# A chain of eight stages on one core: operands of later stages brought and split ahead of their stage

## The reference

```python
x = layernorm(x + L0_attn(x))   # tanh recurrence over 256 steps, 16 heads of state 64
x = layernorm(x + L0_ffn(x))    # router, 8 experts, top 2, gelu
x = layernorm(x + L1_attn(x))   # keys with rope, latent queries, softmax over 128-token chunks
x = layernorm(x + L1_ffn(x))    # router with bias, 64 experts in groups, top 6, gated silu
x = layernorm(x + L2_attn(x))   # gated linear attention, log-sigmoid decay
x = layernorm(x + L2_ffn(x))    # router with bias, 160 experts, top 8, silu
x = layernorm(x + L3_attn(x))   # 6 transformer layers with linear attention, own weights each
x = layernorm(x + L3_ffn(x))    # layer norm with gain, then attention with heads of 16
```

## Time and profile before

| | |
|---|---|
| median of 3 runs | 2036.42 us (2035.14 to 2037.17) |
| profiled execution, its time | 2036.34 us |
| its span, first to last instruction | 2034.6 us |
| PE busy | 1728.0 us, 85% |
| DVE busy | 1585.6 us, 78% |
| ACT busy | 1251.1 us, 61% |
| POOL busy | 348.9 us, 17% |
| mean granted TensorE clock | 0.871 |

### The profile page before, as it was taken

One profiled execution on the slowest core, in us unless ns is written; L12 is line 12 of the kernel. 1 busy time (PEld: TensorE's weight loads), 2 busy tenths in 40 slices (PEclk: granted clock), 3 DMA queues, 4 the chain that ended last, 5 costly groups with the idle time before them and its releaser, 6 DMA issues. The chain is left out here.

```text
span 2034.6 us, 46173 instructions
## 1 busy us (share of the span) xinstructions
PE 1728.0 (85%) x16491; PEld 1083.0 (53%) x16498; DVE 1585.6 (78%) x3793; ACT 1251.1 (61%) x3209; POOL 348.9 (17%) x464
## 2 busy tenths in 40 slices
PE   5999969846859999947759999999968999999585
PEld 5999944435633444425544444444436666665453
DVE  4444459878878999967878999999967787777774
ACT  5666637723526655555438888888856666665465
POOL 1000001000011111110001212222113443443211
PEclk7555569978968999978989999999979999999798
DMA  3000007210004443300006666666620000000100
GB/s 79 10 4 4 4 15 271 88 43 1 0 14 171 154 171 149 141 17 1 0 12 232 232 232 225 224 226 229 232 87 22 22 1 22 21 1 1 36 2 22
DMA packets 51670, 174.06 MB, mean 86 GB/s; under 512 B 7104, under 2 KB 32448, under 8 KB 34112
## 3 DMA queue, kind: packets, MB, share of 16 engines
q1 hardware_dynamic: 50368, 170.09, 23.3%
q10 hardware_dynamic: 1152, 1.90, 0.3%
HBM read 167.45 MB, written 2.95 MB: 84 GB/s over the span
## 5 line engine op out<-in xcount | busy, mean ns | idle before, releaser
L861 DVE TENSOR_TENSOR ps<-ps,m_comb 128x512 f32<-128x512 f32 x520 | 363.1, 699 | 23.9 <-DMA m_comb<-m_shares 7.2
L846 DVE TENSOR_TENSOR m_hwlo<-ps,m_hwhi 128x512 f16<-128x512 f32 x520 | 353.5, 680 | 0.3
L822 ACT ACTIVATE m_hwhi<-ps 128x512 f16<-128x512 f32 x520 | 308.3, 593 | 20.8 <-DVE ps L861 19.4
L828 ACT ACTIVATE ps<-ps 128x512 f32<-128x512 f32 x388 | 225.9, 582 | 80.7 <-PE ps L778 80.5
L778 PE MATMUL ps<-x_hi,m_whi 128*128 128x512 f16 x652 | 250.3, 384 | 8.2 <-DVE m_hwlo L846 4.2
L778 PE MATMUL ps<-x_lo,m_whi 128*128 128x512 f16 x652 | 250.0, 383 | 0.0
L778 PE MATMUL ps<-x_hi,m_wlo 128*128 128x512 f16 x652 | 249.7, 383 | 0.0
L759 POOL CAST m_whi<-m_stage 128x256 f16<-128x256 f32 (+1 forms) x130 | 55.2, 424 | 907.2 <-PE ps L784 637.6
L461 DVE TENSOR_TENSOR rn_s_lo<-rn_s_full,rn_s_hi 128x32 f16<-128x32 f32 x512 | 98.4, 192 | 131.5 <-ACT rn_s_full L418 131.5
L784 PE MATMUL ps<-m_hwhi,m_whi 128*128 128x512 f16 x520 | 197.4, 380 | 0.3 <-DVE m_hwlo L846 0.2
L784 PE MATMUL ps<-m_hwlo,m_whi 128*128 128x512 f16 x520 | 197.3, 379 | 0.0
(11 more groups left out here) (451 smaller groups left out, 3983.8 us busy)
## 6 DMA issues: line engine op xcount, KB each, us to landing
m_comb<-m_shares SPq DMA_DIRECT2D x128, 1024.0 KB, 5.1
m_stage<-in_m_w SPq DMA_DIRECT2D x97, 128.0 KB, 4.6
m_stage<-in_m_w SPq DMA_DIRECT2D x33, 192.0 KB, 4.7
lj_w<-in_lj_w SPq DMA_DIRECT2D x6, 1024.0 KB, 5.1
lq_w<-in_lq_w SPq DMA_DIRECT2D x1, 1600.0 KB, 6.9
la_w<-in_la_w SPq DMA_DIRECT2D x1, 1280.0 KB, 5.3
rn_rows<-in_L_attn_rows SPq DMA_DIRECT2D x4, 256.0 KB, 4.5
rn_xs<-rn_xn_hi SPq DMA_DIRECT2D x32, 32.0 KB, 1.9
```

The lines of the kernel that those rows point to most:

```text
L822: nc.scalar.activation(hw_hi[:, k % HB, :], weighted(k), ACT.Copy).then_inc(hi_done, 1)
L828: nc.scalar.activation(acted(k), ps[:, 4, :] if gated else bank(k), func).then_inc(act_done, 1)
L846: nc.vector.tensor_tensor(hw_lo[:, k % HB, :], weighted(k), hw_hi[:, k % HB, :], ALU.subtract)\
L861: nc.vector.tensor_tensor(weighted(k), bank(k), comb[:, s, n * QW:(n + 1) * QW], ALU.mult)\
```

## The change

Tiles that last over several stages are made in `build`. Two routers' tiles last from start to end. An early group holds the other routers' weights and all operands of `l1_attn` and `l2_attn`, with room for the split parts; it is closed before stage 5 (`l2_ffn`). A late group then holds the first weights of `l3_attn` and the operands of `l3_ffn`. Nothing that is computed changes.

- All early tiles are requested by SP at the end of its list in `l0_attn` (15 transfers, 2.6 MB), behind the recurrence's own.
- `l0_ffn`'s POOL list gets four instructions at its end: the cast and subtraction of `la_w` (2560 columns) and of `lg_w` (772).
- `l2_ffn`'s SP list gets 7 transfers, 2.9 MB (`lj_w` of layer 0, `lj_cols`, `lj_own`, `lq_w`, `lq_cols`, `lq_vb`, `lq_sel`) behind the first three units' weights; its POOL list gets the cast and subtraction of the first 1536 columns of `lj_w`.
- `l3_attn`'s POOL list gets `lq_w`'s 3200 columns in seven pieces (six of 512, one of 128), at steps 26 and 29 of each group of the last layer.
- What these instructions did in the later stages goes: transfers, waits, splits.

```diff
+            for name in kept:                                   # l0_attn, SP, after its own transfers
+                sp.dma_start(S.kept[name][:], A[name]).then_inc(kept_got, 16)
+            sp.wait_ge(kept_got, 16 * len(kept))
...
-        sp.dma_start(self.wr[:], self.w_router).then_inc(self.got, 16)        # Router
-        pe.wait_ge(self.got, 16 if self.bias is None else 32)
...
+            for dst, src in loads:                              # experts_phase, SP
+                sp.dma_start(dst, src).then_inc(loaded, 16)
             sp.wait_ge(route.stored, 16 * len(route.turns))
...
+            if loads:                                           # experts_phase, POOL, after all units
+                pool.wait_ge(loaded, 16 * len(loads))
+            for n, (full, hi, lo) in enumerate(later):
+                nc.gpsimd.tensor_copy(hi, full).then_inc(split_hi, 1)
+                pool.wait_ge(split_hi, U + n + 1)
+                nc.gpsimd.tensor_tensor(lo, full, hi, ALU.subtract).then_inc(split_done, 1)
...
-                pe.wait_ge(parts_s, 2)                          # l1_attn and l2_attn
-                dve.wait_ge(got, 96)
-                split_on(dve, parts_s, 1, w_hi[:], w_lo[:], w[:]).then_inc(parts_s, 1)
...
-            act.wait_ge(got, 32)                                # l3_attn
-            dve.wait_ge(got, 32)
-            for n in range(3):
-                split(0, n)
+            def split_ahead(n):
+                run = slice(4 * n * P, min(4 * (n + 1), 25) * P)
+                nc.gpsimd.tensor_copy(ahead[1][:, run], ahead[0][:, run]).then_inc(ahead_high, 1)
+                pool.wait_ge(ahead_high, n + 1)
+                nc.gpsimd.tensor_tensor(ahead[2][:, run], ahead[0][:, run], ahead[1][:, run], ALU.subtract)\
+                    .then_inc(ahead_low, 1)
...
+                if layer == DEPTH - 1 and step in STEP["split"][0:2] and piece_n < 7:
+                    split_ahead(piece_n)
+                    piece_n += 1
...
-            pool.wait_ge(w_got, 16)                             # l3_ffn, POOL in its layer norm
-            nc.gpsimd.tensor_copy(w_hi[:], w[:]).then_inc(w_hi_s, 1)
-            pool.wait_ge(w_hi_s, 1)
-            nc.gpsimd.tensor_tensor(w_lo[:], w[:], w_hi[:], ALU.subtract).then_inc(w_lo_s, 1)
...
+          ExitStack() as early, ExitStack() as late):           # build
+            if k == "5":
+                early.close()
+                keep(late, ("lj_w", [P, 2, 16 * P], F32), ...)
```

More of the change, by code:

```diff
@@ L59, with layernorm_phase @@
     pass
-def layernorm_phase(nc, S, src, dst, eps=LN_EPS, gain=None, shift=None, out=None, sync=None, pool=None, ready=None):
+def layernorm_phase(nc, S, src, dst, eps=LN_EPS, gain=None, shift=None, out=None, sync=None, pool=None):
     rows_in, stats_s, aggr_s, std_s, rstd_s, shift_s, normed_dve, normed_act, back, stored, turned, high_s = S.sems.new(
@@ L226, in l0_attn @@
             "load_ident", "load_identb", "rnn_a_got", "rnn_b_got", "rnn_c_got", "rnn_o_got")
+        kept_got = S.sems.new("kept_got")
+        kept = [name for name in S.kept if not name.endswith(("_hi", "_lo"))]
         rows_got = [S.sems.new(f"load_rows{g}") for g in range(4)]
@@ L675, in experts_phase @@
     comb_got = [S.sems.new(f"{tag}_comb_got{s}") for s in range(UB)]
+    loaded = S.sems.new(f"{tag}_loaded")
     x_hi, x_lo = S.x_hi, S.x_lo
@@ L1582, in sb @@
             return ctx.enter_context(nc.sbuf_tensor(name, shape, dt))
-        x0, cols, own = sb("lj_x0", [P, N]), sb("lj_cols", [P, DEPTH, 5]), sb("lj_own", [P, P])
-        w = sb("lj_w", [P, 2, WN])
-        w_hi, w_lo = sb("lj_whi", [P, 2, 12 * P], F16), sb("lj_wlo", [P, 2, 12 * P], F16)
+        x0 = sb("lj_x0", [P, N])
+        w, w_hi, w_lo, cols, own = (S.kept["lj_" + n] for n in ("w", "whi", "wlo", "cols", "own"))
+        ahead = [S.kept["lq_" + n] for n in ("w", "whi", "wlo")]
         mix, mix_hi, mix_lo = sb("lj_mix", [P, P]), sb("lj_mixhi", [P, P], F16), sb("lj_mixlo", [P, P], F16)
@@ L1993, in split @@
                 nc.gpsimd.tensor_scalar(quarter[0], quarter[1], 2.0, cols[:, c:c + 1], ALU.mult, ALU.add)
-            pool.wait_ge(w_got, 16)
-            nc.gpsimd.tensor_copy(w_hi[:], w[:]).then_inc(w_hi_s, 1)
-            pool.wait_ge(w_hi_s, 1)
-            nc.gpsimd.tensor_tensor(w_lo[:], w[:], w_hi[:], ALU.subtract).then_inc(w_lo_s, 1)
-            nc.gpsimd.memset(v[:, :, :, :, DH:DH + 1], 1.0).then_inc(w_hi_s, 1)
-            pool.wait_ge(w_lo_s, 1)
-            pool.wait_ge(w_hi_s, 2)
-        layernorm_phase(nc, S, S.xT, S.rT, gain=cols[:, 0:1], shift=cols[:, 1:2], sync=load, pool=split, ready=(cols_got, 16))
+            pool.wait_ge(cleared, 1)
+            nc.gpsimd.memset(v[:, :, :, :, DH:DH + 1], 1.0).then_inc(cleared, 1)
+            pool.wait_ge(cleared, 2)
+        layernorm_phase(nc, S, S.xT, S.rT, gain=cols[:, 0:1], shift=cols[:, 1:2], pool=clear)
         def weight(n):
@@ L2274, in build @@
         for k in STAGES:
+            if k == "5":
+                early.close()
+                keep(late, ("lj_w", [P, 2, 16 * P], F32), ("lj_whi", [P, 2, 12 * P], F16), ("lj_wlo", [P, 2, 12 * P], F16),
+                     ("lj_cols", [P, 6, 5], F32), ("lj_own", [P, P], F32), ("lq_w", [P, 25 * P], F32),
+                     ("lq_whi", [P, 25 * P], F16), ("lq_wlo", [P, 25 * P], F16), ("lq_cols", [P, 10], F32),
+                     ("lq_vb", [P, P], F32), ("lq_sel", [P, P], F32))
             stages[int(k)](nc, S, A)
```

142 lines of the change are left out of this document (61 added, 81 removed).

## The result

The changed kernel takes 2012.36 us (median of 4 runs, 2008.56 to 2013.46) against 2035.78 for the kernel before (4 runs, 2034.92 to 2037.17): a ratio of 0.9874, 95% interval 0.9862 to 0.9886 (the two medians alone give 0.9885). The gain is 23.4 us where 32.9 was forecast, and 2012.36 lies above the range's upper end of 2010. The profiled execution took 2013.46 us with a span of 2011.7, 22.9 less than the span before.

The account below looks back on a forecast made before the run. PE was taken as the bound in dense middles, with idle stage starts to shorten: 1.5 + 2.2 + 3.9 + 11.6 + 4.2 + 4.6 + 6.5 - 1.6 = 32.9 us, from 2036.34 to 2003.4 us; range 1997.5 to 2010.

Parts of the forecast that it names:

- The end of 1.2: In `l0_attn`, 2.6 MB beside the recurrence: priced at nothing, 1.2 us kept as the end if transfers slowed by a tenth.
- it stays up (0.06): Rival: shorter pauses leave PE at its upper clock, router logits at most halve, up to 9.5 us more, 1994; chance 0.06.
- stays down for 74 us (0.02): Rival: the clock stays low for 74 us in `l2_ffn`, losing the 32.9 gained and 4 more, 2041; chance 0.02.
- the 4.6: Start of `l3_attn`: DVE no longer waits for `lj_own` and begins once PE has turned four tiles, all 4.6 us gained.
- `l1_ffn`'s router: Start of `l1_ffn`: without the small transfer PE begins when the block does, gaining 2.2 us.
- the covers: Dense stretches of `l0_ffn` and `l2_ffn` meant to hide POOL's moved splits: cost nothing, DVE keeps its 0.68 us.
- the rival of 2009: Next wait comes sooner: `l2_attn` loses 1.1 us, pieces 2.2, two larger starts a fifth; some 27 us gained, chance 0.12.
- 11.6 expected: Start of `l1_attn`: transfers and split gone, DVE's own clearing is the last wait, 11.6 us gained; ends 11.3 and 12.1.
- 4.1 of 4.2: Start of `l2_attn`: ACT waits only for POOL's second clearing, 4.2 us gained; 3.1 if DVE slows POOL.
- 6.3 of 6.5: Layer norm of `l3_ffn`: DVE no longer stands behind POOL's splitting, 6.5 us gained; ends 5.9 and 6.7.
- The last layer's pieces: Last layer of `l3_attn`: three split pieces before group 2's x_hi delay PE, 1.6 us lost; ends 0 and 2.2.
- `l2_ffn`'s router and its loads: Start of `l2_ffn`: PE begins with the block, 3.9 us gained; the 2.9 MB of early loads there cost nothing.

Follow-up runs that it names:

- burst_alone: The kernel before plus only the early-transfer burst, 13 transfers (2.5 MB) into tiles that nothing reads; 2039.82 us, ratio 1.0011 to the kernel before.
- the first pair: The first profiles of the kernel before and of the changed kernel, nothing edited; medians 2035.78 and 2012.36 us.
- before_again: The kernel before run once more for a second profile, nothing edited; 2036.70 us, ratio 0.9999 to the kernel before.
- warm_pe: The changed kernel plus 30 unread 512-column matmuls in PE's pauses at the start of `l3_attn`; 2005.78 us, ratio 0.9847 to the kernel before.
- the second comparison: The changed kernel run once more, nothing edited, against the kernel before; 2010.40 us against 2037.68, ratio 0.9871.
- clear_on_pool: The changed kernel with the clearing at the start of `l1_attn` moved from DVE to POOL; 2010.20 us, ratio 0.9865 to the kernel before.

## Why the forecast came out 9 us short

The stage lengths of all profiles, each kernel counted only where its edit does not reach. Three profiles have the old stages, `burst_alone` among them (for the first row two), and six to eleven the new ones; the first row has the seven with the whole burst:

| stage, with the norm ahead | forecast | before, us | after, us | difference of means |
|---|---|---|---|---|
| `l0_attn` | 0 | 267.3 to 267.6 | 268.1 to 270.0 | +2.0 |
| `l0_ffn` | -1.5 | 128.0 to 128.2 | 127.0 to 128.0 | -0.7 |
| `l1_attn` | -11.6 | 176.1 to 178.8 | 163.8 to 166.2 | -12.1 |
| `l1_ffn` | -2.2 | 305.4 to 306.6 | 304.0 to 304.8 | -1.5 |
| `l2_attn` | -4.2 | 150.6 to 153.0 | 147.2 to 147.9 | -4.1 |
| `l2_ffn` | -3.9 | 470.2 to 472.2 | 466.8 to 468.2 | -3.9 |
| `l3_attn` | -3.0 | 389.9 to 391.3 | 388.1 to 388.4 | -2.2 |
| `l3_ffn` | -6.5 | 131.0 to 131.4 | 124.6 to 127.6 | -5.2 |
| sum | -32.9 | | | -27.6 |

**The step that failed: "if they slowed it by a tenth it would be 1.2. I take nothing".** The load beside the recurrence was priced as a slight slowing of its transfers. What it delayed was PE's own work: 1.5 to 1.9 us of standstill in six of seven profiles, 1.6 to 2.0 us over the recurrence's steps, +2.0 in the stage's mean, and the standstill gone with one wait on SP. The end of 1.2 was too low as well.

**The step that was missing: no term for the clock after a shorter start.** Every saving was taken at the durations of the trace before, and the only clock rivals were that it stays up (0.06) or stays down for 74 us (0.02). It did something smaller: the shorter starts did not always bring the full clock forward by as much.

- In `l0_ffn` this shows in every profile. PE started with the block and 1.5 us were gained up to the first logits. But the full clock comes 12.6 to 14.4 us after the first expert product in the eleven profiles after, and 11.5 to 12.1 in the three of the old stage. Behind that point the lead is 0.5 us in the first pair and 0.7 in the means, so 0.8 went back.
- In `l3_attn` DVE started 4.6 us sooner and the next 20 us kept that. In the first pair the first products then ran at 0.56 instead of 1.00, and 1.1 of the 4.6 were gone. Against `before_again` it is 1.0, but against `burst_alone`, which has the old start and met the lower clock too, nothing is lost: 0.6 in the means.
- In `l3_ffn` the norm gave 6.3, and in the first pair PE's first products met 0.51 for 0.68: PE started 25.85 us sooner than before (1885.67 against 1911.52) and 5.3 us later was 25.06 ahead (1890.98 against 1916.04), which is 0.8 lost. In the means of all profiles it is 0.3 there, and another 0.8 at the stage's end.

`warm_pe` shows for `l3_attn` that the lower clock is what costs. For the other two it rests on the rows.

**`l1_ffn`'s router gave 1.5 of 2.2.** PE's first logits were 2.2 us earlier. The next term is DVE beside POOL, which the forecast looked for in the covers and not here: the router's copy takes 0.40 to 0.82 us in all eleven profiles after and 0.18 in the three of the old stage, and by the router's end 1.9 us are left in the means. The other 0.4 go up to where the full clock comes, as in `l0_ffn`.

**What remains is scatter.** In the last stage the clock fell 12.8 us before the last norm in the first profile and 3.8 us before it in the second: 2.2 us on the same instructions. Over all profiles it fell more than 9 us ahead in six of eleven after and in none of three before; whether the change made that likelier can't be told from so few. The Trainium skill (TensorE: Matmul & The Clock Gate, What's actually happening) says that the number of slow matmuls at a start differs between runs of one kernel; this pair agrees: in `l0_ffn` the full clock came 13.8 and 12.6 us after the first expert product. That the moment of its fall differs too is seen in the rows above. The stages' means give 27.6 us, the second comparison gives 27.3, and the first, with the changed kernel's four runs by chance somewhat high, 23.4. So some 5.3 of the 9.5 us are located by the table: 2.0 in the recurrence, some 3 at the lower clock and 0.3 in the router's copy. The other 4 are what runs of one kernel differ by. The measured time lies nearest to the rival of 2009, but that is chance: POOL lost 0.15 us at `l2_attn` and not 1.1, and the two larger starts, 11.6 and 6.5, gave 12.2 and 6.3. In the forecast's own arithmetic the high ends add up to 36.1 and not 36.2, and half of the three logits (7.0, 7.1 and 6.0 us) is 10.0 and not 9.5; neither changes anything.

**Right, by their own steps.** `l1_attn`: DVE behind its own clearing, 11.6 expected, 12.2 at ACT's first copy (416.94 for 427.20, while the norm ahead began 1.93 later than before); `clear_on_pool` confirms the next wait 0.5 us behind. `l2_attn`: 4.1 of 4.2, by POOL's clearing, which kept its pace. The norm: 6.3 of 6.5. The last layer's pieces: 1.4 us of PE's wait, 1.7 in the stage, 1.6 forecast, with the mechanism and the place. `l2_ffn`'s router and its loads: 3.9 of 3.9 in the mean, so those 2.9 MB were indeed hidden. The covers: POOL's last moved subtraction in `l0_ffn` ended at 387.73, 7 us before PE, and PE's lead over the kernel before, 0.52 us, is the same ahead of the moved splits (at 325 us) and beside them (at 386).

## What to carry to other kernels

Transfers moved beside a long chain of small instructions are not free because their data is not awaited: a full load of the DMA engines can hold up PE itself, most likely by its instructions, which the queue view shows arriving through the same engines. So pace such loads (one wait in the middle was enough) and look for idle time that "issue" ended. Price a shorter start together with the clock's level that its work will meet, and where a start is a chain with pauses, try filling PE's pauses: 30 matmuls that nothing reads gained 4.4 us in one profile and some 3 in another, where the clock fell in between. When a start moves, look again at which of DVE's instructions now fall beside POOL's. A program that scatters by 5 us needs stage lengths from several profiles, since one pair of profiles put the gain at 22.9 where the means say 27.6.

## What the hardware showed unexpectedly

- A full load of the DMA engines (share 0.88 to 0.98 from 60 to 66 us) stopped PE for 1.5 to 1.9 us in a part of the kernel that waits for no transfer, in seven of eight profiles with the burst; 1.3 MB, a wait, and 1.1 MB did not.
- A DVE instruction on 4 columns with two inputs in SBUF took 2.72 and 4.33 us beside POOL's work on 3200 columns, and 256 columns took 3.6 us beside POOL's clearing of 4096; each ended with POOL's instruction, within 0.2 us. A DVE instruction that reads PSUM kept its 1.33 us, and POOL nearly kept its own times (6.24 against 6.25 us, 3.66 against 3.51).
